# Two joints of a four-layer kernel: batch norms taken into the MLP's rounds, and the last batch's finish rewritten on ScalarE and VectorE

## What is computed

```python
# MLP: RMS norm, 128 -> 512, gelu, 512 -> 128, added to its input y
# seam, per batch u:   X[u] = X[u] + layernorm(Y[u])     (X: the residual)
#                      n[u] = layernorm(X[u])            (input of the experts)
# experts:             enc = sigmoid(n @ enc_W); cont = enc @ s2c_W
#                      gates = top 2 of 8 from tanh(cont @ rW1) @ rW2
#                      moe = sum over e of gate_e * (relu(cont @ We1[e]) @ We2[e])
#                      dec = sigmoid(sigmoid(moe @ c2s_W) @ dec_W)
#                      e = layernorm(dec) * ln_g + ln_b
#                      out[u] = X[u] + layernorm(e)
```

## Time and profile before

| | us |
|---|---|
| median of 3 runs | 1348.86 (1348.03 to 1349.47) |
| the profiled execution | 1345.07 |
| its span | 1343.2 |
| MLP, first H matmul to the last statistics | about 830 to 956 |
| experts, block start to the end | about 956.5 to 1343.2 |

### The profile page before, as it was taken

The page is one execution under the profiler, slowest core; times in us unless marked ns, Lnnn a source line. Parts: engine busy times, 40 slices in busy tenths (PEclk is TensorE's granted clock), DMA queues, the critical chain, the costliest instruction groups (busy, mean ns, idle before and its releaser), DMA issues. The chain is left out here.

```text
span 1343.2 us, 27695 instructions
## 1 busy us (share of the span) xinstructions
PE 1178.1 (88%) x7410; PEld 527.0 (39%) x7410; DVE 941.6 (70%) x2955; ACT 915.7 (68%) x1369; POOL 658.8 (49%) x1101
## 2 busy tenths in 40 slices
PE   4989999999999999996999298999579999999992
PEld 1222222222222222223666196777324343443431
DVE  5677777777777777675788874666356788888752
ACT  3878999999999999994555761333435666666553
POOL 5425655555565556433555341222333565666445
PEclk7999999999999999998999698999779999999997
DMA  5664565555555555506910030000000000000000
GB/s 157 135 117 101 97 109 111 107 101 103 110 108 101 104 101 98 108 1 179 268 39 0 0 127 1 0 0 0 0 0 1 9 17 8 16 8 16 17 17 24
DMA packets 71681, 87.95 MB, mean 65 GB/s; under 512 B 10352, under 2 KB 65174, under 8 KB 66006
## 3 DMA queue, kind: packets, MB, share of 16 engines
q1 hardware_dynamic: 69582, 85.94, 30.1%
q10 hardware_dynamic: 2024, 1.12, 0.4%
HBM read 63.84 MB, written 31.59 MB: 71 GB/s over the span
## 5 line engine op out<-in xcount | busy, mean ns | idle before, releaser
L561 ACT ACTIVATE a_probs<-a_S 128x1024 f32<-128x1024 f32 x512 | 496.7, 1036 | 52.4 <-DVE a_S L707 45.0
L707 DVE TENSOR_TENSOR a_S<-a_S,a_tables 128x256 f32<-128x256 f32 (+1 forms) x512 | 281.2, 560 | 144.8 <-PE a_S L577 141.8
L584 PE MATMUL a_O<-a_probs,a_V 128*32 128x512 f32 x2048 | 274.5, 608 | 2.4 <-ACT a_probs L561 0.6
L577 PE MATMUL a_S<-a_Qs,a_Ks 48*128 48x512 bf16 x1024 | 180.0, 388 | 15.8 <-ACT a_probs L561 11.0
L577 PEld LDWEIGHTS a_S<-a_Qs,a_Ks 48*128 48x128 bf16 x1024 | 42.7, 93 | 230.9 <-ACT a_probs L561 194.2
L2189 ACT ACTIVATE e_hid<-e_H 128x512 f32<-128x512 f32 x128 | 69.5, 594 | 58.7 <-PE e_H L2295 58.7
L454 POOL CAST a_parts<-a_whole 128x512 bf16<-128x512 f32 x45 | 27.5, 611 | 151.1 <-DVE a_whole L717 151.1
L1939 ACT ACTIVATE g_hid<-g_H,w_b 128x512 f32<-128x512 f32 x64 | 44.0, 687 | 83.1 <-PE g_H L1962 83.1
L2293 PE MATMUL e_H<-e_gated,w_We 64*128 64x512 f32 x256 | 74.2, 656 | 1.3 <-ACT e_hid L2189 1.2
L584 PEld LDWEIGHTS a_O<-a_probs,a_V 128*32 128x32 f32 x2048 | 40.4, 108 | 82.3 <-issue 67.2
L2304 PE MATMUL e_O<-e_hid,w_We 128*64 128x512 f32 x256 | 69.8, 616 | 0.4 <-ACT e_hid L2189 0.4
(11 more groups left out here) (370 smaller groups left out, 2394.0 us busy)
## 6 DMA issues: line engine op xcount, KB each, us to landing
a_parts_dram<-a_parts SPq DMA_DIRECT2D x94, 192.0 KB, 5.5
a_Qs<-a_parts_dram SPq DMA_DIRECT2D x60, 192.0 KB
m_taps_by_step<-h_taps SPq DMA_DIRECT2D x8, 1024.0 KB, 13.4
m_taps<-m_taps_by_step SPq DMA_DIRECT2D x8, 1024.0 KB, 5.0
a_Qs<-a_parts_dram SPq DMA_DIRECT2D x60, 128.0 KB
a_Ks<-a_parts_dram SPq DMA_DIRECT2D x30, 192.0 KB
a_Qs<-a_parts_dram SPq DMA_DIRECT2D x68, 64.0 KB
XY<-L_attn_x SPq DMA_DIRECT2D x16, 256.0 KB, 6.9
```

Source lines behind the costliest of these rows:

```text
L561: act.activation(probs[n % KEPT][:], S[n % RING][:], ACT.Exp).then_inc(exped, 1)
L577: mm = pe.matmul(S[n % RING][:, par, :], Ks[p][rows, pr, kb * P:(kb + 1) * P], Qs[p][Q_OF(kb)][rows, pr, :], start=True, stop=True)
L584: mm = pe.matmul(O[VC * j:VC * (j + 1), :], V[q][:, kb, HG * g + j, :], probs[(2 * m + j // 2) % KEPT][:, j % 2, :], start=(kb == 0), stop ...
L707: v.tensor_tensor(s[:, :, where], s[:, :, where], wide, ALU.mult).then_inc(corrected, 1)
```

## The change

1. In the MLP, VectorE's and GpSimd's rounds from t = 4 on are written out. At the end of VectorE's rounds 4 to 12 one piece of work for batches 0, 1, 2 is added, three pieces per batch: the moments of the output (GpSimd inverts them), the norm and sum (`join`), and the moments of the sum (GpSimd inverts them).
2. In the MLP's last round VectorE computes mean and variance of batches 3 to 14 ahead of its wait for OUT, ScalarE loads the table of Sqrt, takes the root and loads the table of Sigmoid, and VectorE inverts after the last sum. The last batch's statistics move into the experts, where GpSimd inverts them.
3. The experts start with VectorE forming xn of batch 0 itself.
4. Round 19 of the experts goes, and round 18 loses `shapes`. The last batch is finished by `close`: VectorE does gain, bias, both norms and the sum, ScalarE two roots (after a table load in round 17), and the output goes out in two halves from the SP and the ScalarE queue.

```diff
+        X, FIRST, LOOPED = core.X, core.FIRST, 4
+        ahead = Norm(core, ctx, "g_ahead", sb("ahead_st", [P, 2 * FIRST, NT, 6]), affine=False, deep=2 * FIRST)
+        of_output, of_sum = (lambda u: 2 * u), (lambda u: 2 * u + 1)
+        turn_of_output, turn_of_join, turn_of_sum = (lambda u, k=k: LOOPED + 3 * u + k for k in range(3))
+        measured, rooted = sem("measured"), sem("rooted")
+        mean, var, root = (sb(n, [P, B, NT]) for n in ("mean", "var", "root"))
+        later = slice(FIRST, B - 1)
+        joins_by = lambda u: turn_of_join(u) + 1 + 2 * u
+        BULK = B - 1 + 2 * FIRST
+        ROOTS = BULK + 8
...
-            with pool.Fori(0, B // 2 - 1) as i:
+            with pool.Fori(0, LOOPED // 2) as i:
                 for p in range(2):
                     body(i * 2 + p, p, i)
+            for t in range(LOOPED, B):
+                if t + 2 < B:
+                    power.invert(pool, t + 2, rstd)
+                for u in range(FIRST):
+                    if t == turn_of_output(u):
+                        ahead.invert(pool, of_output(u), ahead.rstd, of_output(u))
+                    if t == turn_of_sum(u):
+                        ahead.invert(pool, of_sum(u), core.xrstd, of_sum(u), to=u)
...
+            act.preload_act_table(ACT.Sqrt)
+            act.wait_ge(measured, ROOTS)
+            act.activation(root[:, later], root[:, later], ACT.Sqrt).then_inc(rooted, 1)
+            act.preload_act_table(ACT.Sigmoid)
...
-                if not isinstance(t, int):
+                if not isinstance(t, int) or t + 2 < B:
                     power.squares_of(v, t + 2, Y[:, t + 3])
+                if last:
+                    measure_later()
                 OUT[p].read(v, i + 1)
                 y = Y[:, t + 1].rearrange("p c d -> p (c d)")
                 OUT[p].emptied(v.tensor_tensor(y, y, OUT[p].t[:], ALU.add))
                 OUT[p].after(v, i + 1)
-                for c in range(NT):
-                    v.bn_stats(core.yst[:, t + 1, c], Y[:, t + 1, c])
-
-
-            with v.Fori(0, B // 2 - 1) as i:
+                if last:
+                    return
+                for c in range(NT):
+                    op = v.bn_stats(core.yst[:, t + 1, c], Y[:, t + 1, c])
+                op.then_inc(measured, 1)
+
+            def join(u):
+                k = of_output(u)
+                v.wait_ge(ahead.inverted, (k + 1) * Norm.INVERT)
+                for c in range(NT):
+                    op = v.tensor_scalar(Y[:, u + 1, c], Y[:, u + 1, c], ahead.neg[:, k, c:c + 1], ahead.rstd[:, k, c:c + 1],
+                                         ALU.add, ALU.mult)
+                op.then_inc(measured, 1)
+                v.wait_ge(measured, joins_by(u) + 1)
+                v.tensor_tensor(X[:, u], X[:, u], Y[:, u + 1], ALU.add).then_inc(measured, 1)
...
+            def measure_later():
+                v.wait_ge(measured, BULK)
+                moments(v, tick, core.yst[:, FIRST + 1:B], mean[:, later], var[:, later], root[:, later])
+                tick.mark(v.tensor_scalar(root[:, later], var[:, later], 1e-5, None, ALU.add))
+                assert tick.start + tick.n == ROOTS
+
+            def settle_later():
+                v.wait_ge(rooted, 1)
+                tick.step(v.reciprocal(core.in_rstd[:, later], root[:, later]))
+                tick.mark(v.scalar_tensor_tensor(core.in_mean[:, later], mean[:, later], -1.0, core.in_rstd[:, later],
+                                                 ALU.mult, ALU.mult))
+
+            with v.Fori(0, LOOPED // 2) as i:
                 for p in range(2):
                     body(i * 2 + p, p, i)
-            body(B - 2, 0, B // 2 - 1)
-            body(B - 1, 1, B // 2 - 1, last=True)
+            for t in range(LOOPED, B):
+                body(t, t % 2, t // 2, last=(t == B - 1))
+                for u in range(FIRST):
+                    if t == turn_of_output(u):
+                        ahead.moments_of(v, of_output(u), Y[:, u + 1], p=of_output(u))
+                    if t == turn_of_join(u):
+                        join(u)
+                    if t == turn_of_sum(u):
+                        v.wait_ge(measured, joins_by(u) + 3)
+                        ahead.moments_of(v, of_sum(u), X[:, u], core.xmean, p=of_sum(u), to=u)
+            settle_later()
...
-        joined.start = 7
+        LAST = FIRST - 1
+        joined.start = -LAST * Norm.MEASURE
...
+        GAINED, BIASED, MOVED, CLOSED = (PER * B + n for n in (2, 3, 4, 6))
+        CHAIN = Norm.MEASURE * B
+        roots = sb("roots", [P, 2, NT])
...
-                        joins=within(0, B - 4), shapes=within(3, B + 2), ends=within(4, B + 3))
+                        joins=within(0, B - 4), shapes=within(3, B + 1), ends=within(4, B + 2),
+                        closes=isinstance(i, int) and i == B + 1)
...
-            for i in range(B - 4, B + 4):
+            for i in range(B - 4, B + 3):
...
-            sp.wait_ge(stored, 16 * B)
+            sp.wait_ge(steps, CLOSED)
+            sp.dma_start(out[:, B - 1, 0:NT // 2], X[:, B - 1, 0:NT // 2]).then_inc(stored, 16)
+            sp.wait_ge(stored, 16 * (B + 1))
...
-            add(0, 0)
-            add(1, 0)
-            joined.invert(pool, 0, core.xrstd)
-            layer_norm(0)
-            joined.invert(pool, 1, core.xrstd)
-            add(2, 0)
+            pool.sem_inc(summed[0], FIRST)
+            pool.sem_inc(joined.inverted, LAST * Norm.INVERT)
             pool.wait_ge(TP.full, FIRST_XT)
...
-                if isinstance(i, int) and i == 0:
-                    joined.invert(pool, 2, core.xrstd)
...
+                if c and not closes:
...
+            joined.invert(pool, LAST, rstd, to=B - 1)
...
-            act.wait_ge(ready, 1)
-            act.activation(tmp[:], tmp[:], ACT.Sqrt).then_inc(ready, 1)
-            act.preload_act_table(ACT.Sigmoid)
-            act.wait_ge(ready, 4)
-            for u in range(3):
-                normalise(u, rstd, shift, normed[0])
+            act.sem_inc(normed[0], FIRST)
...
+                    if isinstance(i, int) and i + 3 == B - 1:
+                        act.wait_ge(ready, 1)
...
+                if closes:
+                    act.preload_act_table(ACT.Sqrt)
+                    root(0, decoded)
                 if shapes:
                     shaped.wait(act, i - 3)
                     normalise(i - 3, shaped.rstd, shaped.offsets, normed[2])
+
+            def root(k, norm):
+                act.wait_ge(norm.steps, norm.start + CHAIN)
+                act.activation(roots[:, k], norm.var4[:, B - 1], ACT.Sqrt, scale=0.25).then_inc(normed[1], 1)
 
             act.wait_ge(W.folded, W.MERGED)
             take_xT(FIRST_XT)
             for m in range(HC):
                 spikes_encoded(1, m)
             rounds(act, body)
+            root(1, shaped)
+            act.wait_ge(steps, CLOSED)
+            act.dma_start(out[:, B - 1, NT // 2:NT], X[:, B - 1, NT // 2:NT]).then_inc(stored, 16)
...
+            def close(u):
+                y, x = Y[:, u + 1], X[:, u]
+                last = Tally(v, steps, start=PER * B)
+                for c in range(NT):
+                    op = v.scalar_tensor_tensor(y[:, c], y[:, c], decoded.neg[:, u, c:c + 1], W.gain[:], ALU.add, ALU.mult)
+                last.mark(op)
+                v.wait_ge(normed[1], B)
+                last.step(v.reciprocal(decoded.rstd[:, u], roots[:, 0]))
+                assert last.start + last.n == GAINED
+                for c in range(NT):
+                    op = v.scalar_tensor_tensor(y[:, c], y[:, c], decoded.rstd[:, u, c:c + 1], W.bias[:], ALU.mult, ALU.add)
+                last.step(op)
+                assert last.start + last.n == BIASED
+                shaped.moments_of(v, u, y)
+                for c in range(NT):
+                    op = v.tensor_scalar(y[:, c], y[:, c], shaped.neg[:, u, c:c + 1], None, ALU.add)
+                last.mark(op)
+                assert last.start + last.n == MOVED
+                v.wait_ge(normed[1], B + 1)
+                last.step(v.reciprocal(shaped.rstd[:, u], roots[:, 1]))
+                for c in range(NT):
+                    op = v.scalar_tensor_tensor(x[:, c], y[:, c], shaped.rstd[:, u, c:c + 1], x[:, c], ALU.mult, ALU.add)
+                last.mark(op)
+                assert last.start + last.n == CLOSED
...
-                    v.wait_ge(summed[0], 3)
-                    joined.moments_of(v, 2, X[:, 2], core.xmean)
+                    v.wait_ge(joined.inverted, FIRST * Norm.INVERT)
+                    v.tensor_tensor(shift[:, B - 1], joined.neg[:, LAST], rstd[:, B - 1], ALU.mult).then_inc(ready, 1)
...
-            prepare = Tally(v, joined.steps)
-            moments(v, prepare, core.yst[:, 1:B + 1], mean[:], var[:], tmp[:])
-            v.tensor_scalar(tmp[:], var[:], 1e-5, None, ALU.add).then_inc(ready, 1)
-            v.wait_ge(ready, 2)
-            v.reciprocal(rstd[:], tmp[:]).then_inc(ready, 1)
-            v.wait_ge(ready, 3)
```

(18 more changed lines are left out.)

16 lines of the change are left out of this document (9 added, 7 removed).

## The result

| | us |
|---|---|
| before, median of 4 runs | 1348.44 (1346.53 to 1349.47) |
| after, median of 4 runs | 1329.76 (1325.02 to 1335.36) |
| ratio after / before | 0.9865, 95% interval 0.9846 to 0.9885 |
| forecast for after | 1333.8 (1327 to 1341) |
| profiled execution after | 1335.36, its span 1333.6 |

The kernel is faster by 18.7 us; 15.1 were forecast. The after kernel spreads over 10 us and the one before over 3 (over 4 to 8 in the later groups, so that a wide spread isn't the changed kernel's alone). So the two profiles are 9.7 apart and not 18.7: 5.6 of the 9.0 in between are the after profile's distance to its median, 3.4 that of the one before.

What follows compares the result with a forecast made beforehand. TensorE's period through a closed chain bounds MLP rounds, its idle stretch the experts' start, one batch's chain the end. Terms -15.0 (experts' start), -9.5 (end), +9.4 (MLP) sum to -15.1: 1348.86 to 1333.8 us, 8 in 10 1327 to 1341.

Steps and rivals of the forecast that it cites:

- The MLP, +9.4 forecast: VectorE's added moments and joins delay the transposes in nine MLP rounds: 9.4 us lost, bounds 6 to 15.4.
- Rival C: In the MLP the new work costs its full price, 15.4 us, no slack left: 1339.8 us; chance 0.15.
- D: Rival: GpSimd's added MLP inversions come into series with those the scaling needs, costing 31.3 us: 1355.7 us; chance 0.04.
- Written-out code at nothing: In the MLP, the 12 written-out rounds are more code but were costed at nothing.
- roots and tables hidden: In the MLP's last round, ScalarE's table loads and root are over at 955.0, before VectorE's last sum at 955.40.
- The seam, -13.2 forecast: At the experts' start, transposes come 12.9 us earlier and the way to the encoder takes 0.3 less: 13.2 gained.
- Rounds 0 and 1, -1.8 forecast: First experts rounds: 0.4 us gained from less VectorE and GpSimd work, 1.4 from TensorE's clock (bounds 0 and 6).
- Rival E: At the seam, round 0 or 1 waits for batch 3's norm, sum and moments: some 8 us back; chance 0.05.
- A: The forecast itself, 1333.8 us, expecting most of the lower clock in experts rounds 0 and 1 again; chance 0.60.
- B: Rival: TensorE's lower clock in experts rounds 0 and 1 is mostly gone, 5 us more gained: 1329 us; chance 0.16.
- The end, -9.5 forecast: Last batch's finish on VectorE and ScalarE brings the last sum from 1340.41 to 1330.9: 9.5 us gained, range 8.5 to 11.
- The collision: At the end, GpSimd's addition of batch 14 meets VectorE's moments of the last batch and delays a small step: 1.0 us.

Runs made afterwards that it cites:

- group e: First group of follow-up runs, on another chip than the later two groups; its shared runs of the kernel before have a median of 1348.67 us.
- group g: Third group of follow-up runs, with and without short filling matmuls; its shared runs of the kernel before have a median of 1347.99 us.
- e4: Changed kernel with the nine MLP pieces moved ahead of VectorE's wait for OUT; 1320.61 us, ratio 0.9803.
- f4: Kernel before with VectorE's and GpSimd's MLP rounds from 4 on written out and nothing added; single run, 1346.27 us.
- e3: Changed kernel with the end put back as before, so MLP and seam changes alone; 1342.62 us, ratio 0.9951.
- g2: Repeat of e4, the changed kernel with the pieces ahead of VectorE's wait for OUT; 1323.15 us, ratio 0.9820.
- e1: The changed kernel run again without edits, for a second profile and its spread; 1331.17 us, ratio 0.9862.
- f3: Changed kernel without GpSimd's last addition for batch 14, so that batch's output is incomplete; single run, 1330.69 us.
- f1: Changed kernel with short unread matmuls on TensorE around the first transposes and in rounds 0 and 1 of the experts; 1332.64 us, ratio 0.9884.
- g1: e4's kernel with short matmuls: seven ending the MLP, five ahead of the experts' wait, three after the first transposes, others in rounds 0 and 1; 1319.36 us, ratio 0.9794.
- f2: Changed kernel with the edits of e4 and f1 together, pieces earlier and short matmuls; 1321.49 us, ratio 0.9801.

## Why the prediction was right, and where it was not

1. **What bounds.** Right in all three places: the closed chain of a round, TensorE's idle stretch at the seam, one batch's chain at the end. The number is in part luck: the stages' differences, with the average of item 5, add up to about 16 us, near the forecast, while the medians gave 18.7 at first, 17.5 in group e and 20.0 in group g. The remaining 1.5 to 4 us lie in no stage that the change touches, and the one profile of the kernel before is 3.4 faster than its median run; what those runs spent more stays open.

2. **The MLP, +9.4 forecast, +8.07 measured.** The mechanism is the forecast one and two of its sizes were a little large. In the rounds behind a piece the period is 8.44, 8.66 and 8.56 instead of 7.66 (moments of the output, join, moments of the sum), so three times 0.78 + 1.00 + 0.90 = 8.04. The transposes came 4.16 and 4.29 after H for the moments (4.38 forecast) and 4.38 for the join (4.67 forecast). The scaling starts 1.53 after the moments began (893.57 less 892.04), not 1.61, as it overlaps their last step; the hand-over to TensorE took 0.06, not 0.1; a join took 1.75 from its start to the scaling's (883.26 to 885.01), not 1.9. The lower bound's half microsecond per piece was not there; 0.1 to 0.2 was. Rival C (15.4) is refuted, D as well: the inversions hold up nothing. Round 0's own variation carries no part of this: behind it the loss is 8.04. That the pieces' place was the whole cost, I had seen only as a chain; e4 made it a result.

3. **Written-out code at nothing, roots and tables hidden.** Right by f4 (rounds of 7.66) and by the seam's rows. The second load is over 0.7 before the last sum ends. On the loads the row was the better guide: the first one ends at 963.37 and the root starts 0.66 later, released by VectorE; the one at the end ends at 1323.48 and its root starts 0.39 later, also released by VectorE. The drain of 1.38 beside the load, which the Trainium skill gives in "ScalarE: Activation LUTs", section "What ACT_TABLE_LOAD costs", is larger than either gap, so the trace doesn't bear it out here. Each load begins 0.02 after the instruction ahead of it or later, with nothing drained behind it either. After the second load ScalarE had no work, so that one tells nothing. (With a drain of 1.38 the second table would have ended at 955.0 + 1.38 = 956.4 by the prediction's own times, not at 956.7.)

4. **The seam, -13.2 forecast, -12.92 measured.** The block started 1.0 after the last sum, as worked out, and xn took 1.16 (1.1 forecast) to 968.52. But the transposes began 0.46 after xn, and no memset held them, neither the one I had named (L2104 in the earlier trace rows) nor L189, which the bracket names: TensorE's list has eight semaphore instructions and a row of waits at the block's start, and the last of these is over at 968.92. That term stood at 0.1 in the prediction. First transposes 2.7 after the last sum instead of 2.2; from there to the encoder 1.40 instead of the 1.56 of the sum, which gave 0.2 back. (The 3.6 from the last sum to the encoder, in the part on what would show it, should have been 3.8 by the same sum; measured 4.1.)

5. **Rounds 0 and 1, -1.8 forecast.** This is the step that the profile shows wrong and the average shows about right. E0 to C2 is 39.7 before and 39.6 and 39.8 in the two kernels with the old seam. With the new one it is 41.10, 39.35, 38.04, 35.83, 38.26, 35.85 and 35.66 in the seven without fillers, on average 37.7: 2.0 gained. Rival E, 8 us back in these rounds, is refuted by the same seven. The step that failed is the one before the number: I had argued as if the clock were a property of the code, with A and B as its two outcomes. The same code gets either, from execution to execution (41.10 and 35.66), and the median of the first runs, 4 us below the forecast, lies nearer to rival B's 1329 than to A. What decides it in an execution stays open; the start alone doesn't, since e3 and g2, with H0 at 833.31 and 833.39, have 38.04 and 35.85. How the 2.0 divide between the clock (1.4 in the sum) and the shorter list of round 0 (0.4) the runs don't separate: at a like clock, 0.73 before and 0.74 in e1 and f3, the stage is 0.4 to 1.4 shorter. The bounds of this part were also added up wrongly: 13.2 + 1.6 + 6 is 20.8, not 19, which makes the lower end 1323 instead of 1325.

6. **The end, -9.5 forecast, -10.01 measured.** Gain, root, bias and moments went as forecast, with smaller hand-overs: the moments are done 5.5 after the last decode, not 5.8. The collision came at its forecast size, 1.0, but on another instruction: batch 14 was normalised 5.45 after the last decode (1327.63 less 1322.18), not 4.9, and GpSimd's addition then met the subtractions and not the moments. One of the four began 0.11 after the addition, at 1327.91, and ended 0.08 after the addition did. The half microsecond is batch 14's inversion: the five steps after the power took 0.22, 0.34, 0.34, 0.30 and 0.34, where the earlier trace rows have 0.20 for such a step. The Trainium skill says in "SBUF — State Buffer", section "Who interferes with whom", that whichever starts second waits for the other, and I had given up to 1 us to its working on batch 14's inversion, at 0.2 apiece. The trace agrees for the one subtraction, which took 1.28 and waited out the addition, and it agrees that the inversion's steps suffer, at some 0.1 apiece, but that time lay under VectorE's chain, and the end came no later for it. The tail from the last sum was 2.75 instead of 2.79: two queues bring nothing that can be read here.

7. **Not forecast.** C2 to C15 is 0.5 to 1.0 us longer in all kernels with the new seam (268.51 to 268.99) and at 268.13 to 268.29 in the two without it, against 267.97 before. The cause stays open; nothing in these rounds' code changes. So does what sets H0.

## What to carry to other kernels

Work that is added to an engine with idle time costs by its place in the list: look which wait in a round the engine reaches early, and put the new work ahead of that one, as far as the idle time there reaches (1.6 us here, for pieces of 1.5 to 1.8). Here the same nine pieces cost 8 us behind VectorE's wait for OUT and nothing ahead of it, and that version (1320.6 and 1323.2) beats both kernels; with short filling matmuls it came to 1319.4, 29 us below before, of which the fillers' own share is 1.2 to 3.8.

Where TensorE's clock lies at the lower level behind an idle stretch, filling matmuls raised it, but they pay only where the engine really has nothing to do. Behind a wait that is already met they are on the path (f1 lost 3.8 at the seam, the five of g1 still 0.5), and a bracket names the last releaser, which need not be what the engine was held by: read what it did in that time, and what value the kernel waits for. And a comparison whose stages contain such a stretch needs several executions of each kernel, since the same code gave spans of 1326.2 to 1335.1; cut the span at the same instructions and compare stages.

## What was not expected of the hardware

- Four subtractions on VectorE with one tensor and one scalar column each took 1.87 us beside GpSimd's addition and 0.87 without it; one of them took 1.28 instead of 0.28, the other three lost nothing. In the forecast only steps with two tensor operands stood to lose. GpSimd's addition itself took 1.31 instead of 1.26.
- TensorE at the lower clock for some 30 us (969.5 to 1000.3) in an execution in which it was busy 5.4 to 7.2 of every 8 us, and going back and forth between the levels, 0.79 to 0.98 in the same windows, in another one with the same code and the same busy time. From E0 to C2 that is 41.10 against 35.66 us, and 32.58 where the clock was full throughout (f2).
- With short matmuls in front the encoder group ran at the full clock (1.88 for what takes 3.78 otherwise). In g1 the clock then fell in an idle time of 2.70 us, and in f2, with one of 2.71 at the same place, it stayed at 1.00.
- Eight semaphore instructions in a row at the start of a block cost TensorE 0.15 us each, 1.2 us on the way to its first matmul, and the profile's bracket put that time down to a memset.
